# Moving the eighth piece of the first feed-forward product ahead of the first tile's products with V

## Time and profile before

| What | Value |
|---|---|
| median of 3 runs | 2046.94 us |
| the profiled execution's own time | 2050.78 us |
| span of the profiled execution | 2049.0 us |
| PE busy | 1999.8 us, 98% of the span |
| DVE busy | 1738.7 us, 85% |
| ACT busy | 1293.0 us, 63% |
| GpSimd busy | 317.5 us, 15% |
| line 1086 (first feed-forward product), x2400 with kept weights | 276.8 us busy, mean 273 ns |
| line 1785 (gelu), x480 | 243.4 us busy, mean 560 ns |

### The profile page before, as it was taken

How to read it: one execution, slowest core, us unless ns; L and a number is a source line. 1 busy time by engine, 2 the same in 40 slices (tenths; PEclk the granted TensorE clock), 3 DMA queues, 4 the chain that set the end, 5 groups by cost and what they waited for, 6 DMA issues and landing times.

```text
span 2049.0 us, 64453 instructions
## 1 busy us (share of the span) xinstructions
PE 1999.8 (98%) x27206; PEld 1424.3 (70%) x27206; DVE 1738.7 (85%) x3687; ACT 1293.0 (63%) x2081; POOL 317.5 (15%) x329
## 2 busy tenths in 40 slices
PE   5889999999999999999999999999999999999999
PEld 4767667777666777766777766667776677777676
DVE  7778889888888888888988888888888898888771
ACT  7775566676555677656667656667765666766452
POOL 1011111111111111111111111111111111111110
PEclk8999999999999999999999999999999999999999
DMA  6776666777666677766667766667777666776656
GB/s 217 161 193 194 177 178 182 199 197 196 177 194 171 189 198 195 185 190 189 173 194 202 199 174 186 181 181 202 192 195 184 191 180 185 199 202 177 181 175 191
DMA packets 403216, 385.42 MB, mean 188 GB/s; under 512 B 256880, under 2 KB 304112, under 8 KB 402928
## 3 DMA queue, kind: packets, MB, share of 16 engines
q1 hardware_dynamic: 401296, 381.12, 68.1%
q10 hardware_dynamic: 1632, 0.18, 0.1%
HBM read 232.32 MB, written 22.54 MB: 124 GB/s over the span
## 4 chain that ended last, share of the span: by engine, by line
PE 81%; SPq 4%; DVE 4%; ACT 4%; DMA 3%; issue 2%; POOL 0%; ACTq 0%; DVEq 0%
PE F L1149 19%; PE F L1086 16%; PE B L892 9%; PE B L1053 8%; PE sc L892 7%; PE YT L924 6%; PE YT L892 3%; DMA y<-ygT 3%; PE YT L976 3%; SPq L2044 2%; PE sc L954 2%; PE YT L995 2%; PE YT L1086 1%; PE F L847 1%; PE YT L1025 1%
## 5 line engine op out<-in xcount | busy, mean ns | idle before, releaser
L1149 PE MATMUL F<-ring,hT 128*128 128x512 f16 x1984 | 467.7, 379 | 0.5 <-issue 0.5
L1149 PEld LDWEIGHTS F<-ring,hT 128*128 128x128 f16 x1984 | 189.1, 98 | 198.4 <-issue 0.8
L1086 PE MATMUL F<-xT,kept 128*128 128x256 f16 x2400 | 276.8, 273 | 2.0 <-issue 1.2
L892 PE MATMUL B<-mix,WT 128*128 128x256 f16 x2304 | 267.5, 273 | 0.0
L1785 ACT ACTIVATE hT<-F,b,f_rho 128x256 f16<-128x256 f32 x480 | 243.4, 560 | 37.8 <-PE F L1086 37.7
L1086 PEld LDWEIGHTS F<-xT,kept 128*128 128x128 f16 x2400 | 234.6, 98 | 42.1 <-issue 2.6
L892 PEld LDWEIGHTS B<-mix,WT 128*128 128x128 f16 x2304 | 222.7, 98 | 33.3 <-DVE gT L1389 0.3
L279 DVE SCALAR_TENSOR_TENSOR mixf<-dx,maa,xnT 128x256 f32<-128x256 f32 x512 | 238.7, 527 | 0.1
L1742 ACT ACTIVATE Shl<-S 128x256 f16<-128x256 f32 x128 | 53.1, 415 | 236.2 <-PE YT L995 125.8
L1988 POOL TENSOR_TENSOR Shl<-S,Shl 128x256 f16<-128x256 f32 x128 | 89.2, 697 | 708.5 <-ACT Shl L1742 702.1
L1736 ACT ACTIVATE att<-att 128x512 f16<-128x512 f32 x256 | 147.5, 624 | 67.7 <-DVE att L1350 67.7
(11 more groups left out here) (208 smaller groups left out, 3108.6 us busy)
## 6 DMA issues: line engine op xcount, KB each, us to landing
ring<-w_dram SPq DMA_DIRECT2D x352, 512.0 KB, 3.7
kx<-kT SPq DMA_DIRECT2D x96, 256.0 KB, 3.8
rx<-rT SPq DMA_DIRECT2D x96, 256.0 KB, 4.5
xa<-in_L_attn_x SPq DMA_DIRECT2D x32, 512.0 KB, 5.0
vbd<-vN SPq DMA_DIRECT2D x256, 64.0 KB, 2.1
x<-in_L_attn_x SPq DMA_DIRECT2D x32, 512.0 KB, 5.0
out<-x SPq DMA_DIRECT2D x31, 512.0 KB, 3.5
kept<-in_L_ffn_W SPq DMA_DIRECT2D x5, 512.0 KB, 12.0
```

What stands on the lines that cost most here:

```text
L892: mm = eng.matmul(out[:, gg * BT:(gg + 1) * BT], WT[:, w, a, kk, rows(g)], mix[:, m % 2, b, kk, :], start=(i == 0 and kk == 0), stop=(i == ...
L1086: mm = eng.matmul(up_place(f, j)[:, i * BT:(i + 1) * BT], w, xT[:, :, kk, :], start=(kk == 0 and a == 0), stop=(kk == G - 1 and a == 1))
L1149: mm = eng.matmul(F[:, t, :], hT[:, k, rows(t)], ring[:, use % RING, i, a * C:(a + 1) * C], start=(k == 0 and a == 0), stop=(k == NH - 1 a ...
```

## The change

In `pe_step`, the eighth piece of the first feed-forward product, `pe_up(n, 7)`, stands before `pe_att_v(n, 0)` instead of behind it. `pe_att_v(n, 0)`, `pe_from_state(n, 0)` and `pe_scores(n, 2)` then stand directly behind each other. No instruction is added or removed, and the other engines' queues are the same.

```diff
         if ff:
             pe_up(eng, n, 6)
+            pe_up(eng, n, 7)
         if att_n:
             pe_att_v(eng, n, 0)
-        if ff:
-            pe_up(eng, n, 7)
-        if att_n:
             pe_from_state(eng, n, 0)
             pe_scores(eng, n, 2)
             pe_prepare(eng, n, "sc2")
```

## The result

The changed kernel takes 2081.08 us, median of five runs (2072.8 to 2086.76), against 2048.63 us for the kernel before, also in five runs (2045.29 to 2051.84). The ratio is 1.0157, 95% interval [1.0139, 1.0175], so the loss is 32 us with an interval of 28 to 36. The direction was forecast; the time lies above the range of 2057 to 2076. The profiled execution took 2077.39 us (span 2075.6), 26.6 more than the profile before, and it is the second fastest of the five.

A forecast was written before the change was run, and what follows sets the result against it. PE's queue was taken to set the time. Pauses of 7.0 us (15 ordinary steps) and 13.0 (13 late), less 0.2 in two steps, gave +19.8 on 2046.94: 2066.7 us, range 2057 to 2076.

The forecast's parts named there:

- What bounds the kernel: PE's queue sets the time, busy 1494.60 of 1500 us in the steady middle; almost nothing there waits.
- Added: a pause of piece 7 for gelu 5: On PE, piece 7 waits for gelu 5: 0.47 us each in 15 steps, 1.00 each in 13.
- G: The end of gelu 5 on ACT; piece 7 was to start 0.14 us after it.
- Removed: one hand-over on PE: One switch fewer between full-size pieces and small tiles on PE: gain 0.10 us a step, 3.0 over 30 steps.
- Bounds: Only the number of late steps can move: all ordinary gives 13.0 us, all late 27.8.
- B: Late steps turn ordinary because y's transfer lands in time: +8.9 us, 2055.8 us; chance 0.08.
- A: Gelu 5 is done in time, so only the hand-over on PE counts: -3.0 us, 2043.9 us; chance 0.04.
- C: Ordinary steps turn late and piece 6 also waits for gelu 4: +35.3 us, 2082.2 us; chance 0.06.
- the split into 13 and 15: Of 30 steps, 13 late (joining of y waits for its transfer), 1.00 us each, and 15 ordinary, 0.47 each.
- D: Pauses lower PE's clock to 1.2 GHz for piece 7 and V products: +83 us, about 2150; chance 0.02.
- What is queued behind: PE's later products start equally late; DVE's idle time grows, other engines and ring refills cost nothing; lost time isn't caught up.

The follow-up runs named there:

- the pause without the run: Kernel before, in its old order, with one added wait: the first tile's V products wait until gelu 5 is done; 1.0088, +18 us.
- the run without the pause: Against the kernel before, piece 7 moved behind the third scores, so 144 small matmuls run on and piece 7 needs no pause; 1.0036, +7.4 us.

## Why the prediction missed

- *What bounds the kernel*: right. PE's queue sets the time; everything lost there was lost for good.
- *Added: a pause of piece 7 for gelu 5*: right in mechanism and size. Release at G + 0.14, V products 1.84 and state products 1.12 later, as in step 4 above. Without the gain of the hand-over the pauses were reckoned at 22.8 us. In the profile piece 7's pause is 21.2, and all pauses ahead of the V products together grew by 19.9, since the waits of piece 6 shrank by 1.3.
- *Removed: one hand-over on PE*: this is the step that failed. The gain itself came, 3.0 us. But the step said "State products and third scores follow each other before and after, and what is behind them is unchanged", and put what the new neighbours cost at nothing. It priced only the switch between kinds and not the run that arises: 144 small matmuls, 288 instructions with their weight loads, in the 1.92 us that it takes unstalled, with a block of instructions due in it in some steps. In the profile that cost 12.3 us, in eleven steps, and it is the term that is missing from +19.8: 19.9 + 12.3 - 3.0 = +29.2. The trace of before held the hint: the only two places with "issue" in the steady part, 0.5 us each, one of them in the state products. I left them out of the bounds.
- *Pause and run together*: not thought of. The pause makes more blocks late: PE's same queue stalls 12.2 us in 11 places with it and 4.4 in 5 without it, and the whole change then costs only +2.6. The comparison with the other two kernels, +18 with the pause without the run, +7.4 with the run without the pause, +32 with both, shows less, since the pauses of the first were shorter.
- *Bounds*: "The one term that can move is how many steps are late" was wrong, and with it the upper end of 2076. The lower end does not fit the text either: the range is said to take in most of B, and B's own time, 2055.8, lies under 2057.
- *Rivals*: A was out, since the pause came; the saved switch is real but lost in the stalls. B and C did not come: 13 pauses of piece 7 are of 0.57 us or more and 15 at most 0.45, so the split into 13 and 15 held, though not in the same steps. 35 waits less the 28 of piece 7 leave 7 for piece 6, about as many as before. That C's time, 2082, is the measured one is luck. D did not come at pauses of up to 1.0 us.
- *What is queued behind*: right. DVE's idle time before line 1400 grew in step 4 from 1.03 to 1.58 us, and PE waited for nothing of DVE's or of a transfer.

## What to carry to other kernels

When a change of order on a saturated TensorE queue brings small matmuls together, count the instructions in the run and the time that the array needs for them, and look for "issue" in the waits. Instructions come in blocks, and small matmuls can use one up in less time than the next needs to come: at 1.92 us for 144, the 128 matmuls of a block take an estimated 1.7 us, and in step 4 it was 2.6 to 3.1 us from the start of the packet to the end of the stall. Ask first of any moved consumer of a double buffer when its buffer is read out, by laying the reader's queue beside it; here that one comparison gave the pause to within 3 us. A pause can cost more than its length when many small instructions follow soon after it: keep full-size work behind a wait, and small runs away from it. But do not pay for that with a longer pause, as the kernel that waited ahead of piece 6 did.

## What the runs showed that was not expected

Stalls of 0.7 to 1.5 us inside a run of like matmuls in the changed kernel (up to 2.4 in the others), with no semaphore. Put 12 matmuls in at the start of the program, and all those that were found again within a run moved by exactly 12. A block comes as one packet of 16.4 KB, which took 0.9 to 1.3 us in the two cases shown. The granted clock held at 1.00 under some 28 pauses of up to 1.0 us. It fell to 0.98 over the steady part when they were 2.4 us on average (66.9 / 28) and up to 3.5, because in 18 of 30 steps the matmuls right behind the pause ran for a while at 0.50, the 1.2 GHz level.
